# A gated layer of 8 experts: rows beyond two whole pieces packed, and some down products on unsplit operands

## The chip, the cores and the metric

One core of one Trainium2 chip runs the whole kernel in one launch. The metric is device time in microseconds. Before: 599.43 us, the median of three runs (598.75 to 601.22).

## The reference, cut to what matters

Four blocks of a gated cross-attention network over x (1024 tokens of 128 numbers, here kept as 128 partitions by 1024 columns). Each block has an attention-like part and a feed-forward part. The change touches the feed-forward part of the second block, called layer 1 in the code:

```
logits = xt @ Wg.T                       # 8 experts
w, idx = top_k(softmax(logits), 2);  w = w / w.sum()
cw[token, idx] = w                       # 1024 x 8, two non-zero per token
h = silu(xt @ W1[e].T) * (xt @ W3[e].T)  # per expert, 352 hidden rows
y = sum over e of cw[:, e] * (h @ W2[e].T)
x = x + tanh(g_ffn[1]) * y
```

All eight experts are computed for all tokens, and the gate rows (the weights of each expert per token, the tanh factor in them) make the sum.

## The kernel before, in words

Every engine has its own instruction stream, written out by hand, and the streams meet through semaphores. PE multiplies, ScalarE (ACT) and VectorE (DVE) work on what it leaves in PSUM, GpSimd (POOL) does some side work, and SP issues nearly all DMAs on one queue.

**Steps.** The class `Moe` (L41) holds a layer's plan: a list of steps (expert, piece, half). For layer 1 (L100) a piece is 128 hidden rows, the third one 96 (352 = 128 + 128 + 96); a half is 512 tokens. The order is expert by expert: three pieces of the first half, three of the second. Experts 6 and 7 share a tail: both first halves, then both second ones. That is 48 steps. `lag` (L78) gives the step at which so many half-steps have passed since an expert was done, and so times the work on splits, gates and sums.

**A step.** PE's `up` (L717) makes two products (W1, W3) of one piece, each in three passes on split operands: the fp32 value is written as a high part of type fp32r and a low part, and high*high, high*low and low*high are added (`products`, L708, its matmul on L713). Then ACT's `hidden` (L1116, L1132) takes silu of the first into `h_act`, DVE's `product` (L1579, L1586) multiplies by the second, ACT's `high` (L1146) and DVE's `low` (L1600, L1609) split the result, and PE's `down` (L749) multiplies by the piece of W2 in three passes, into the expert's two PSUM banks. PE runs `up` three steps ahead of `down`. `up(s)` waits for `product(s-2)`, since two pairs of PSUM banks alternate.

**Weights.** Two slots in SBUF hold two experts' W1, W3 and W2. SP's `load` (L355, issue on L363) fills a slot once both of the old expert's low parts are made; ACT makes the high part (`split_hi_up` L958, `split_hi_down` L971), DVE the low part (`split_lo` L1544, L1548), at steps set by `next_weights`. The first two experts' low parts are POOL's, in the attention before.

**Gates.** Routing runs on DVE between its first steps; PE turns the weights (`turn_gates`, L780, after down 5), ACT copies them to SBUF, SP writes them to DRAM (L427) and reads each expert's row back to all 128 partitions (`spread`, L382, issue on L384), eight of them, and only then issues the load of expert 4. DVE's `gate` (L1611, L1621) multiplies an expert's output by its row into `y_g`, `accumulate` (L1623, L1629) adds it to x, 1024 columns at once. Experts 6 and 7 go through `finish` (L1551, multiply on L1567, add on L1568) per half. A down product of expert e + 2 waits for the gate of e, which frees its banks.

**The end of the layer.** The next norm's products (L452, L459, L469) stand behind downs 42, 43 and 44, the `features` products of the next block (L646) behind down 46. They wait for the last `product` and for the norm. Then the pair sums begin: ACT's tanh over sums that DVE (L1468) and POOL make. DVE runs the two finishes of the second half between its pair sums (L1434, L1436), and PE's next mean, and ACT's square of it (L915), wait for them.

**Layer 2** behind it has the same up products (L739 to L741), and its down product (L756) is one matmul on fp32 operands that aren't split; the compiler makes it two instructions in the trace.

Of the kernel before, what the change touches and what calls it, by code (L numbers as in the profile page):

```python
# [25 lines left out]
P = 128  # L26
B, S = 16, 64
T = B * S
# [12 lines left out]
class Moe:  # L41
# [4 lines left out]
    def __init__(self, layer, experts, hidden, gated, slots, topk, ahead, orders, routed=None):  # L46
        self.layer, self.experts, self.gated, self.slots, self.topk, self.ahead = layer, experts, gated, slots, topk, ahead
        self.routed = routed or experts
        self.hidden = hidden
        self.chunks = [(f, min(P, hidden - f)) for f in range(0, hidden, P)]  # L50
        self.up = hidden * (2 if gated else 1)
        self.width = self.up + P * len(self.chunks)
        self.steps = []
        for kind, group in orders:
            pieces = range(len(self.chunks))
            if kind == "halves":
                self.steps += [(e, k, t) for t in range(2) for e in group for k in pieces]
            else:
                self.steps += [(e, k, None) for e in group for k in pieces]
# [4 lines left out]
        self.begin = [b - a for a, b in zip(size, self.end)]  # L64

# [34 lines left out]
    Moe(1, 8, 352, True, 2, 2, 3, [("halves", [e]) for e in range(6)] + [("halves", [6, 7])]),  # L100
# [20 lines left out]
def flamingo(nc, a, out):  # L121
    ctx = ExitStack()
    with ctx:
# [97 lines left out]
        table = sb("table", [P, 1])  # L221
        h_part = [h_act[:, i // 2, (i % 2) * HALF:(i % 2 + 1) * HALF] for i in range(4)]
# [21 lines left out]
        def down2(e):  # L244
# [22 lines left out]
              + ["wlu_first"] + (["scaled", "sel"] if m.layer == 2 else ["hi", "lo", "whd", "wld", "wld_first", "gate", "acc"]) + ["xn"] * (m.layer == 3)} for m in MOES]  # L267
# [44 lines left out]
        def acc_bank(m, e):  # L312
            return 4 if m.layer == 2 else 4 + 2 * (e % 2)
# [35 lines left out]
        def _(sp):  # L349
# [5 lines left out]
            def load(m, e):  # L355
# [5 lines left out]
                dst = w_f32[:, u * m.width:(u + 1) * m.width]  # L361
                src = a[f"w{m.layer}"][bass.ds(e, 1)].rearrange("e p w -> (e p) w")
# [22 lines left out]

            for m in MOES:
                if m.layer:

                    last = MOES[m.layer - 1]
                    low_ready(sp, last, last.experts - 1, "u")  # L390
                    if m.layer != 3:
                        low_ready(sp, last, last.experts - 1, "d")
# [35 lines left out]
                sp.wait_ge(once["rows"], 16 * nth(m))  # L428
                for e in range(8):
# [11 lines left out]
        def _(pe):  # L441
# [257 lines left out]
            def moe(m, after={}):  # L699
# [4 lines left out]
                def wap(w, e, lo, size, rows=P):  # L704
                    at_col = (e % m.slots) * m.width + lo
# [11 lines left out]
                def up(step):  # L717
# [3 lines left out]
                    if L == 2 and step == 16:  # L721
                        pe.wait_ge(ln["lo"], 2 * L + 2)
                    if not m.gated:
                        if m.freed(step):
                            pe.wait_ge(s["act"], m.freed(step))
                        f, size = m.chunks[k]
# [17 lines left out]
                    f, size = m.chunks[k]  # L744
                    for i in range(2):
                        mm = products([ps[0:size, 2 * sl + i]], e, i * m.hidden + f, size, P, [n_hi[:, half(t)]], [n_lo[:, half(t)]])
                    mm.then_inc(s["hid"], 1)

                def down(step):  # L749
                    e, k, t = m.steps[step]  # L750
                    acc = acc_bank(m, e)
                    if L == 2:
# [3 lines left out]
                        pe.matmul(ps[:, acc + t], down2(e), h_part[step % 16], start=False, stop=(step + 1 == m.last_of(t))).then_inc(s["h_used"], 1)  # L756
                        return
                    pe.wait_ge(s["lo"], step + 1)
                    if step == m.index(e)[0]:
                        low_ready(pe, m, e, "d")  # L760
                    if step == m.index(e, t)[0]:
                        if e == 1:
                            pe.wait_ge(once["gT"], nth(m))
                        if e >= 2:
                            pe.wait_ge(s["gate"], gates_through(m, e - 2, t))
                    f, size = m.chunks[k]
                    ends = {"first": k == 0, "last": k == len(m.chunks) - 1}
# [1208 lines left out]
```

## Time and profile before

| | |
|---|---|
| median of three runs | 599.43 us |
| the profiled execution, its own time | 601.89 us |
| its span | 600.1 us |
| granted PE clock, mean | 0.99 |
| PE / DVE / ACT busy | 566.8 / 447.4 / 415.2 us |
| this layer's products | from 170.88 to 281 us |
| packets moved by DMA | 40.27 MB, mean 67 GB/s |

The profile is of one execution. Starts are in us from the span's start. Matmuls overlap: the time one costs is the distance from its start to the next one's, less than its own duration. A bracket at a row's end is the engine's idle time before it, and what ended it.

### The profile page before, as it was taken

Reading aid. Unit: us, or ns where it says so; the run is one execution under the profiler, and the core shown is the slowest. Engines: PE = TensorE matmul, PEld = TensorE weight load, DVE = VectorE, ACT = ScalarE, POOL = GpSimd, SP = SyncE. Lnnn points to the kernel's source line nnn. Section 1 sums busy time; section 2 is a strip of 40 time slices with the busy share of each in tenths; the row PEclk is TensorE's granted clock in tenths of the full one; section 3 lists DMA queues with packets and bytes.
Section 4 is the critical chain, followed back from the end, with each engine's and each line's share of the span. In section 5 each row is a group of like instructions: output and inputs, shape, how many; then the busy total and the mean of one; then the engine's idle time right before and its main releaser. Section 6 shows DMA issues by size and latency. Waiting matters only on the chain.

```text
span 600.1 us, 8818 instructions
## 1 busy us (share of the span) xinstructions
PE 566.8 (94%) x3305; PEld 394.1 (66%) x3310; DVE 447.4 (75%) x696; ACT 415.2 (69%) x579; POOL 103.8 (17%) x69
## 2 busy tenths in 40 slices
PE   7999999989999999999896989999998999999997
PEld 5688787656677777775230436566545777888886
DVE  4378987588657898987989676766766847787786
ACT  4798999756755556647999765534513858888885
POOL 5400000001200000003989703200000210000000
PEclk9999999999999999999999799999998999999999
DMA  6207210200200811020000024505510110812100
GB/s 237 71 12 307 71 35 2 74 2 2 76 0 4 317 55 58 2 70 1 5 1 1 1 71 120 164 2 153 163 35 2 37 37 0 301 52 72 37 0 35
DMA packets 16782, 40.27 MB, mean 67 GB/s; under 512 B 1834, under 2 KB 6058, under 8 KB 16740
## 3 DMA queue, kind: packets, MB, share of 16 engines
q1 hardware_dynamic: 16740, 39.71, 19.9%
q8 instruction: 26, 0.43, 0.3%
q14 instruction: 16, 0.13, 0.1%
HBM read 39.01 MB, written 0.70 MB: 66 GB/s over the span
## 4 chain that ended last, share of the span: by engine, by line
PE 71%; DVE 14%; ACT 10%; issue 3%; POOL 1%; DVEq 0%; ACTq 0%; POOLq 0%
PE ps L713 38%; ACT work L1094 6%; PE ps L756 4%; PE ps L452 3%; DVE h_lo L1609 2%; PE ps L469 2%; PE ps L739 2%; PE ps L584 2%; PE ps L741 2%; PE ps L555 2%; PE ps L740 2%; PE ps L569 2%; PE ps L459 2%; PE ps L695 2%; DVE h_act L1586 1%
## 5 line engine op out<-in xcount | busy, mean ns | idle before, releaser
L1609 DVE TENSOR_TENSOR h_lo<-h_act,h_hi 128x512 fp32r<-128x512 f32 (+1 forms) x136 | 118.4, 874 | 39.8 <-ACT h_hi L1139 39.0
L713 PE MATMUL ps<-n_hi,w_hi 128*128 128x512 f32 (+1 forms) x232 | 85.4, 402 | 2.0 <-DVE h_act L1586 1.3
L1139 ACT CAST h_hi<-h_act 128x1024 fp32r<-128x1024 f32 (+1 forms) x88 | 75.3, 856 | 14.6 <-PE ps L713 12.1
L713 PE MATMUL ps<-n_hi,w_lo 128*128 128x512 f32 (+1 forms) x232 | 83.0, 391 | 0.0
L713 PE MATMUL ps<-n_lo,w_hi 128*128 128x512 f32 (+1 forms) x232 | 83.0, 391 | 0.0
L1817 POOL TENSOR_TENSOR rstd<-var_eps,minus_half 128x4 f32<-128x4 f32 x16 | 17.5, 1093 | 319.4 <-DVE var_eps L1273 319.4
L713 PE MATMUL ps<-h_hi,w_hi 128*128 128x512 f32 (+1 forms) x184 | 65.5, 398 | 0.1
L713 PE MATMUL ps<-h_hi,w_lo 128*128 128x512 f32 (+1 forms) x184 | 64.0, 390 | 0.0
L713 PE MATMUL ps<-h_lo,w_hi 128*128 128x512 f32 (+1 forms) x184 | 63.9, 389 | 0.0
L1094 ACT ACTIVATE work<-work,p_rest 128x2048 f32<-128x2048 f32 x31 | 59.5, 1998 | 0.4 <-DVE work L1468 0.4
L1132 ACT ACTIVATE h_act<-ps 128x512 f32<-128x512 f32 (+1 forms) x48 | 28.6, 596 | 40.4 <-PE ps L713 40.4
L1844 POOL TENSOR_TENSOR work<-xc,txt 128x2048 f32<-128x2048 f32 x15 | 53.9, 3624 | 7.9 <-ACT xc L1058 6.7
L713 PEld LDWEIGHTS ps<-n_hi,w_hi 128*128 128x128 f32 (+1 forms) x232 | 42.7, 184 | 13.6 <-DVE h_act L1586 2.1
L713 PEld LDWEIGHTS ps<-n_hi,w_lo 128*128 128x128 f32 (+1 forms) x232 | 42.7, 184 | 10.5
L713 PEld LDWEIGHTS ps<-n_lo,w_hi 128*128 128x128 f32 (+1 forms) x232 | 42.8, 185 | 10.0 <-issue 0.5
L1586 DVE SCALAR_TENSOR_TENSOR h_act<-ps,h_act 128x512 f32<-128x512 f32 (+1 forms) x48 | 32.9, 686 | 16.7 <-ACT h_act L1132 16.5
L1125 ACT ACTIVATE h_act<-ps,p_attn 128x512 f32<-128x512 f32 (+1 forms) x44 | 38.6, 878 | 7.3 <-PE ps L713 6.8
L695 PE MATMUL ps<-work,p_rest 128*32 128x512 f32 x256 | 35.0, 626 | 9.1 <-ACT work L1094 7.9
L1125 ACT ACTIVATE h_act<-ps 128x1024 f32<-128x1024 f32 (+1 forms) x44 | 38.1, 867 | 5.7 <-PE ps L713 5.6
L713 PEld LDWEIGHTS ps<-h_hi,w_hi 128*128 128x128 f32 (+1 forms) x184 | 34.4, 188 | 9.4 <-DVE h_lo L1609 1.2
L713 PEld LDWEIGHTS ps<-h_lo,w_hi 128*128 128x128 f32 (+1 forms) x184 | 34.6, 188 | 7.4 <-issue 0.5
L713 PEld LDWEIGHTS ps<-h_hi,w_lo 128*128 128x128 f32 (+1 forms) x184 | 34.5, 188 | 7.4
(234 smaller groups left out, 1023.7 us busy)
## 6 DMA issues: line engine op xcount, KB each, us to landing
work<-g_rows SPq DMA_DIRECT2D x36, 512.0 KB, 6.4
w_f<-in_w SPq DMA_DIRECT2D x20, 512.0 KB, 3.6
w_f<-in_w SPq DMA_DIRECT2D x8, 544.0 KB, 3.6
work<-in_w SPq DMA_DIRECT2D x2, 512.0 KB, 4.3
work<-g_rows SPq DMA_DIRECT2D x4, 256.0 KB, 9.7
p_rest<-in_p_rest SPq DMA_DIRECT2D x1, 714.0 KB, 9.8
p_attn<-in_p_attn SPq DMA_DIRECT2D x1, 546.5 KB, 6.9
x<-in_xT SPq DMA_DIRECT2D x1, 512.0 KB, 3.6
```

What stands on the lines that cost most here:

```text
L452: pe.matmul(ps[:, LNBANK[j, t][0]], cen_w, x[:, half(t)], start=True, stop=True).then_inc(ln["mean"], 1)
L695: mm = pe.matmul(ps[32 * q:32 * q + 32, DOTS[g // B]], l2pad[:, 31 - g:63 - g], pairs[:, g % 6, q * 512:(q + 1) * 512], start=False, stop= ...
L713: mm = pe.matmul(dst[i], wap(wt, e, lo, size, rows), mv[i], start=(first and c == 0), stop=(last and c == 2))
L756: pe.matmul(ps[:, acc + t], down2(e), h_part[step % 16], start=False, stop=(step + 1 == m.last_of(t))).then_inc(s["h_used"], 1)
L1094: act.activation(pairs[:, g % 6], pairs[:, g % 6], ACT.Tanh, bias=l2b[:, 0:1]).then_inc(x2["tanh"], 1)
L1125: act.activation(places(h_act, m, step), src, ACT.Gelu, **kw).then_inc(s["act"], 1)
L1132: act.activation(h_part[step % parts][0:size], ps[0:size, 2 * (step % 2)], ACT.Silu, **kw).then_inc(s["act"], 1)
L1139: act.copy(places(h_hi, m, step), places(h_act, m, step)).then_inc(s["hi"], 1)
L1586: dve.scalar_tensor_tensor(h, ps[0:size, 2 * sl + 1], b3, h, ALU.add, ALU.mult).then_inc(s["mul"], 1)
L1609: dve.tensor_tensor(lo, src, hi.bitcast(F32), ALU.subtract).then_inc(s["lo"], 1)
L1817: pool.tensor_tensor(rstd[:, r], var_eps[:, r], minus_half[:, r], ALU.pow).then_inc(ln["rstd"], 1)
L1844: pool.tensor_tensor(*sum_of(g, xc[:, half(g // B)]), ALU.add).then_inc(x2["sumB"], 1)
```

## The change

Layer 1's experts keep two whole pieces each (256 hidden rows). The 96 rows left over of experts 0 to 3 are put together to 384 rows, three whole pieces, and so are those of experts 4 to 7: two more "experts", 8 and 9, of three pieces. There are 32 + 12 = 44 steps. Experts 0 and 1 go together now (both first halves, then both second), 2 to 7 one by one, 8 and 9 together at the end.

- A packed piece holds rows of two experts. Its hidden values are multiplied by the gate rows **before** the down product (`gate_packed`, on DVE right after `product`), rows of each expert's gate in the partitions of its hidden rows (`spread_packed`, 12 DMAs into `work`). All packed downs add up in one bank per half, and one `finish` per half adds it to x without a multiply.
- The packed downs, and the down of the second piece and second half of experts 2 to 7, are `unsplit`: one fp32 matmul with the fp32 hidden values and an fp32 copy of W2 (`plain_second`, `plain_rest`, two more DMAs ahead of the load of expert 2). No `high` and no `low` for those 18 steps. Experts 8 and 9 have no split of W2.
- Experts 0 and 1 use one PSUM bank each; ACT copies each half's sum to `y_g` (`keep`), and their gates come at steps 13 and 15, their sums at 14 and 16. All eight experts go through `gate` and `accumulate`.
- SP issues load 4 before it waits for the gates, then sends three gate rows, load 5, three, load 6, two, load 7, four packed pieces' rows, load 8, the last two, load 9.
- What stood at steps 41 to 48 stands four steps earlier, and in the pair sums one finish (expert 9) takes the place of two.

The core of the diff:

```diff
+    def unsplit(self, step):
+        e, k, t = self.steps[step]
+        return self.rest > 0 and (e >= self.routed or e >= self.slots and k == 1 and t == 1)
...
-    def who(self, step, quarters, t=None):
-
-        return [e for e in range(self.experts) if self.lag(e, quarters, t) == step]
+    def next_due(self, step, quarters):
+        return [e + self.slots for e in range(self.experts - self.slots) if self.lag(e, quarters - (self.rest > 0 and e == 0)) == step]
...
-    Moe(1, 8, 352, True, 2, 2, 3, [("halves", [e]) for e in range(6)] + [("halves", [6, 7])]),
+    Moe(1, 8, 352, True, 2, 2, 3, [("halves", [0, 1])] + [("halves", [e]) for e in range(2, 8)] + [("halves", [8, 9])], rest=2),
...
+        def gate_packed(eng, m, step):
+            s, (_, _, t) = mo[m.layer], m.steps[step]
+            c = m.packed(step) % 3 + 3 * (m.steps[step][0] - m.routed)
+            h = h_part[step % 4]
+            eng.wait_ge(s["mul"], step + 1)
+            if c < 4:
+                eng.wait_ge(g_rest_in[0], 16 * 8)
+            else:
+                eng.wait_ge(g_rest_in[1], 16 * 4)
+            return eng.tensor_tensor(h, h, g_rest(c, t), ALU.mult)
...
+            def spread_packed(m, c):
+                if c >= 4:
+                    sp.wait_ge(mo[m.layer]["gate"], 4)
+                for e, p0, p1 in m.owners(c):
+                    sp.dma_start(work[p0:p1, c * T:(c + 1) * T], g_rows[m.layer][e:e + 1, :].broadcast_to([p1 - p0, T])).then_inc(g_rest_in[c // 4], 16)
...
-                for e in range(m.slots, 2 * m.slots):
+                for e in range(m.slots, 2 * m.slots + (m.rest > 0)):
                     load(m, e)
                 sp.wait_ge(once["gT"], nth(m))
...
+                if m.rest:
+                    for gates, weights in ((range(3), 5), (range(3, 6), 6), (range(6, 8), 7)):
+                        for e in gates:
+                            spread(m, e)
+                        load(m, weights)
+                    for c in range(4):
+                        spread_packed(m, c)
+                    load(m, 8)
+                    for c in range(4, 6):
+                        spread_packed(m, c)
+                    load(m, 9)
+                    continue
...
-                    pe.wait_ge(s["lo"], step + 1)
-                    if step == m.index(e)[0]:
+                    if not m.unsplit(step):
+                        pe.wait_ge(s["lo"], m.split(step))
+                    elif e >= m.routed:
+                        pe.wait_ge(s["gated"], m.packed(step) + 1)
+                    else:
+                        pe.wait_ge(s["mul"], step + 1)
...
+                        if m.rest and 4 <= step <= 10:
+                            pe.wait_ge(s["kept"], step // 2 - 1)
...
+                    if m.unsplit(step):
+                        pe.wait_ge(plain_in, 32)
+                        c = (e - m.routed) * len(m.pieces(e)) + k
+                        w = plain_rest[:, c * P:(c + 1) * P] if e >= m.routed else plain_second[:, e * P:(e + 1) * P]
+                        pe.matmul(ps[:, acc_bank(m, e, t)], w, h_part[step % 4], start=ends["first"], stop=ends["last"]).then_inc(s["h_used"], 1)
+                        return
...
+                def keep(i):
+                    step = 2 * i + 1
+                    e, _, t = m.steps[step]
+                    act.wait_ge(s["h_used"], step + 1)
+                    act.copy(y_g[:, e, half(t)], ps[:, acc_bank(m, e, t)]).then_inc(s["kept"], 1)
...
                         if m.gated:
-                            if e == 0 and step == m.lag(0, 7):
-                                gate(0, 0)
-                                gate(0, 1)
+                            if e < m.slots and step == 13 + 2 * e:
+                                gate(e, 0)
+                                gate(e, 1)
                             for t in range(2):
-                                if e and step == m.lag(e, 5, t):
+                                if e >= m.slots and step == m.lag(e, 6 if e == 2 else 5, t):
                                     gate(e, t)
-                            if step == m.lag(e, 6 if e else 8):
+                            if step == (14 + 2 * e if e < m.slots else m.lag(e, 7 if e == 2 else 6)):
                                 accumulate(e)
...
                     if g == 3:
-                        finish(MOES[1], 6, 1)
-                    if g == 5:
-                        finish(MOES[1], 7, 1)
+                        finish(MOES[1], 9, 1)
```

## Rows read from the trace of the kernel before

**Rows 1.** The page's first part: busy us (share of the span), instructions.

```profile
PE 566.8 (94%) x3305; PEld 394.1 (66%) x3310; DVE 447.4 (75%) x696; ACT 415.2 (69%) x579; POOL 103.8 (17%) x69
```

**Rows 2.** Stretches of the layer: us, busy (x instructions) by engine, granted clock, DMA.

```profile
200.00:207.00 7.00, 6.39 (x28) 4.77 (x27) 7.00 (x12) 4.10 (x9) 0.00 (x0) 1.00 1.02 389
207.00:217.00 10.00, 10.00 (x44) 7.77 (x44) 9.04 (x15) 6.08 (x12) 0.00 (x0) 1.00 0.30 104
...
171.00:281.00 110.00, 108.05 (x480) 83.30 (x480) 91.89 (x162) 65.29 (x119) 2.39 (x2) 1.00 0.20 69
```

**Rows 3.** The chain that ended last, 170 to 290 us, its longest piece: start, us, what.

```profile
206.49 45.34 PE ps L713 x195
```

**Rows 4.** PE in order of time: start, us, line, tiles [idle before <-releaser].

```profile
170.88 0.47 PE L713 MATMUL ps<-n_hi,w_hi 128*128 128x512 f32 x1
...
190.25 1.04 PE L780 MATMUL ps<-p_first,rt_w 128*8 128x128 f32 x8 [0.61 <-DVE rt_w L1542]
...
206.49 0.50 PE L713 MATMUL ps<-n_hi,w_hi 128*128 128x512 f32 x1 [0.61 <-DVE h_act L1586]
...
265.95 0.48 PE L713 MATMUL ps<-n_hi,w_hi 128*96 128x512 f32 x1 [0.66 <-DVE h_act L1586]
...
278.57 1.88 PE L646 MATMUL ps<-n,p_rest 128*128 128x512 f32 x4
```

**Rows 5.** The chain in the next layer's loop, 396 to 410 us: start, us, what.

```profile
404.58 0.86 PE ps L756 x2
...
406.82 0.86 PE ps L756 x2
```

**Rows 6.** PE in order of time: one product of the first 512 tokens' mean, at 270 us.

```profile
270.31 1.12 PE L452 MATMUL ps<-x,p_first 128*128 128x512 f32 x2
```

**Rows 7.** DVE in order of time, 203 to 211 us.

```profile
203.22 0.88 DVE L1548 TENSOR_TENSOR w_lo<-w_f,w_hi 128x704 fp32r<-128x704 f32 x1
204.02 1.21 DVE L1629 TENSOR_TENSOR x<-x,y_g 128x1024 f32<-128x1024 f32 x1
205.16 0.68 DVE L1621 TENSOR_TENSOR y_g<-ps,work 128x512 f32<-128x512 f32 x1
205.76 0.68 DVE L1586 SCALAR_TENSOR_TENSOR h_act<-ps,h_act 96x512 f32<-96x512 f32 x1
...
210.03 0.55 DVE L1548 TENSOR_TENSOR w_lo<-w_f,w_hi 128x384 fp32r<-128x384 f32 x1
210.50 0.69 DVE L1621 TENSOR_TENSOR y_g<-ps,work 128x512 f32<-128x512 f32 x1
```

**Rows 8.** PE, ACT and DVE behind the last up pass of one step, at 208 us.

```profile
208.00 0.40 PE L713 MATMUL ps<-h_hi,w_hi 128*128 128x512 f32 x1
...
208.20 0.60 ACT L1132 ACTIVATE h_act<-ps 128x512 f32<-128x512 f32 x1 [0.70 <-PE ps L713]
...
208.83 0.69 DVE L1586 SCALAR_TENSOR_TENSOR h_act<-ps,h_act 128x512 f32<-128x512 f32 x1 [0.60 <-ACT h_act L1132]
```

**Rows 9.** Issues on SP's queue, in order of time.

```profile
192.35 0.29 SPq L427 DMA_DIRECT2D g_rows<-gT  x1
194.15 4.14 SPq L384 DMA_DIRECT2D work<-g_rows  x8
```

**Rows 10.** DMA issues: gate rows (192 to 198 us), loads (198 us, 210 us); KB, us to landing.

```profile
DMA to landing us min/median/max: 3.9/7.5/10.1
...
w_f<-in_w SPq DMA_DIRECT2D x1, 544.0 KB, 10.8
...
w_f<-in_w SPq DMA_DIRECT2D x1, 544.0 KB, 3.6
```

**Rows 11.** DVE and ACT in order of time at the start of the pair sums.

```profile
284.10 0.69 DVE L1567 TENSOR_TENSOR ps<-ps,work 128x512 f32<-128x512 f32 x1
284.82 0.69 DVE L1568 TENSOR_TENSOR x<-x,ps 128x512 f32<-128x512 f32 x1
...
290.38 0.60 ACT L915 ACTIVATE sq<-ps 128x512 f32<-128x512 f32 x1 [0.38 <-PE ps L452]
```

More of the change, by code:

```diff
@@ L64, in __init__, with pieces, up_of, width_of @@
         self.begin = [b - a for a, b in zip(size, self.end)]
+    def pieces(self, e):
+        return [(f, min(P, self.sizes[e] - f)) for f in range(0, self.sizes[e], P)]
+    def up_of(self, e):
+        return self.sizes[e] * (2 if self.gated else 1)
+    def width_of(self, e):
+        return self.up_of(e) + P * len(self.pieces(e))
+    def part_of(self, e, part):
+        first = self.start_of(e)
+        return (first, first + self.up_of(e)) if part == "u" else (first + self.up_of(e), first + self.width_of(e))
+    def start_of(self, e):
+        return max(self.up_of(o) for o in range(self.experts)) - self.up_of(e)
+    def unsplit(self, step):
+        e, k, t = self.steps[step]
+        return self.rest > 0 and (e >= self.routed or e >= self.slots and k == 1 and t == 1)
+    def split(self, step):
+        return len([i for i in range(step + 1) if not self.unsplit(i)])
+    def packed(self, step):
+        first = self.index(self.routed)[0] if self.rest else self.total
+        return step - first if step >= first else None
+    def owners(self, c):
+        rows = P * c + np.arange(P)
+        return [(e, *(np.flatnonzero(rows // self.left == e)[[0, -1]] + [0, 1]).tolist()) for e in sorted(set((rows // self.left).tolist()))]
     def index(self, e, t=None):
@@ L1140, in high @@
                         return
-                    size = m.chunks[m.steps[step][1]][1]
+                    size = m.pieces(m.steps[step][0])[m.steps[step][1]][1]
+                    if m.unsplit(step):
+                        return
                     act.wait_ge(s["mul"], step + 1)
@@ L1216, in moe @@
                         copy_values(0, 2 + step // 4)
+                    if m.rest and step in (5, 7, 9, 11):
+                        keep(step // 2 - 2)
                     if step == 3:
@@ L1586, in product @@
                     dve.scalar_tensor_tensor(h, ps[0:size, 2 * sl + 1], b3, h, ALU.add, ALU.mult).then_inc(s["mul"], 1)
+                    if m.packed(step) is not None:
+                        gate_packed(dve, m, step).then_inc(s["gated"], 1)
                 def scale(step):
@@ L1643, in next_weights @@
                     for after, part in ((up_after, "u"), (down_after, "d")):
-                        for e in m.who(step, after):
-                            if e + m.slots < m.experts:
-                                split_lo(m, e + m.slots, part)
+                        for e in m.next_due(step, after):
+                            if part == "u" or e < m.routed or not m.rest:
+                                split_lo(m, e, part)
                 if L == 2:
```

145 lines of the change are left out of this document (90 added, 55 removed).

## The prediction

> **What bounds the kernel now.** First the shares of busy time: TensorE (PE) 94% of the span, VectorE (DVE) 75%, ScalarE 69% [rows 1]. Then the stretches of this layer, 171 to 281 us: PE is busy 108.05 of 110.00 us at a granted clock of 1.00, DVE 91.89, ScalarE 65.29 [rows 2]. So PE bounds the layer, and DVE is near: 9.04 of 10.00 us between 207 and 217 us, and all of 200 to 207 us, where PE fell to 6.39 of 7.00 [rows 2]. The chain says the same, one piece of 195 passes in 45.34 us: 0.2325 us a pass [rows 3]. The PE lines show the stops: 0.61 us for the routing weights, 0.61 and 0.66 us for a DVE product [rows 4]. Counted from the last pass's slot, not its modelled end, each is 0.17 us more; with a small one the four make 2.6 us. What I call the loop runs from 170.88 to the feature products at 278.57 us, 107.7 us; 429 passes take 99.7 of it.
>
> **Part 1, the passes.** Before: 48 steps; ahead of the feature products lie 48 ups of 6 passes and 47 downs of 3, 429. After: 32 main steps and 12 packed, 44. Ups: 264 passes. Of the 43 downs ahead of the features, 17 are unsplit (11 packed, 6 of the main: second piece, second half, experts 2 to 7), 26 split: 78 passes. So 87 passes go, 87 x 0.2325 = 20.2 us. The 17 unsplit downs come in: the next layer has the same form (fp32 operands, 128x128 by 128x512) at 0.86 us, and its step, six passes and one such product, repeats every 2.24 us [rows 5]; 2.24 less 1.40 is 0.84, so nothing is hidden beside it. 17 x 0.86 = 14.6 us. **Part 1: -5.6 us.** A piece of 96 rows is now 128 rows, but a pass of either takes the same slot.
>
> Bounds of the unsplit product: below 0.84; above 1.12, what one takes in this very layer where the first lies behind an fp32r pass [rows 6]. I take 0.86, from 32 in the same pattern. At 1.12 the part is -1.2 us.
> The Trainium skill, page FP8 and Floating Point Precision, section TensorE Precision Notes, has a true fp32 product as four passes through the array. At the pass of this loop that would be 0.93 us and the part -4.4; the trace shows two records and 0.86, and I go by it.
>
> **Part 2, what DVE and ScalarE must do.** In steady state DVE instructions follow each other every 0.60 us (0.61 at most), a split of 704 columns takes 0.80, of 384 0.47, an accumulation 1.14 [rows 7]; so 512 columns are 0.60, 256 0.34, 768 0.87. Over the layer 22 low parts, 4 products, 2 accumulations and the third columns' splits go, 12 packed gates and a 3-us share of others come: DVE has less to do. But the room per step matters, and experts have 4 steps now, not 6. A round from expert 4 on: four products 2.4, three lows 1.8, splits 0.94, two gates 1.2, accumulation 1.14 = 7.5 us against PE's 3 x 2.09 + 2.26 = 8.5 us. That holds, at 88% as before.
>
> It does not hold in steps 13 to 18, where the gates of experts 0 and 1 are caught up. Step by step: 13: product, low, split u4 0.60, two gates 3.00; 14: product, low, accumulation 2.34; 15: product, low, three gates 3.00; 16: product, split d4, accumulation 2.08; 17: product, low, split, gate 2.40; 18: product, low, gate, accumulation 2.94. Together 15.8 us against 12.7 of PE, 3.1 too much. The lead that absorbs it: from the end of up(s) to the start of up(s+2) PE has a down, an up and a down, 2.8 us; the product of s is done 0.83 + 0.69 us after up(s) [rows 8], so 1.3 us of lead. **The burst stops PE for 3.1 - 1.3 = 1.8, with DVE's own write-out 2.0 us**, in place of the 0.8 and 0.9 us stops at 206 and 265 us and the small one. The routing stop stays (its split moves from step 7 to 6, in front of the same weights; 0.1 us shorter). Up(35), expert 9's first, needs the split of step 33, which now follows a product and a packed gate that waits for it: dependent DVE instructions are 0.72 us apart [rows 11]. 0.83 + 0.72 + 0.60 + 0.94 = 3.1 us against PE's 0.70 + 1.40 + 0.86 = 2.96: 0.2 us. **Stops after 3.0, before 2.6: +0.4 us.** Bounds: -1.5 (burst absorbed) to +2.
>
> Added waits: `kept` before downs 4, 6, 8 and 10 stands in front of PE's queue; the copies lie 1.8 us behind up(5), PE gets there after 4.2 us: nothing. ScalarE gains 22 highs' time and loses 4 copies. `gated` replaces `lo`: same distance. Larger first loads lie in the attention before, where the queue is idle: nothing; with that cover gone, their 3.6 us of landing [rows 10]. The tail has all its steps 4 earlier in the same order: nothing.
>
> **Part 3, SP's queue.** Load 4 is now ahead of the gate rows' write and of eight broadcasts, and so waits for DVE's step 9 (196.0 us by the slots above) in place of the gates at 192.35 [rows 9]. The write then goes at 196.4; before, the first broadcast went 1.8 us behind it [rows 9] and the fastest landed 3.9 us after issue [rows 10]. Behind a load of 384 KB (1.0 us at the 389 GB/s of [rows 2], taken as 1.5 with its start) that makes 196.4 + 1.5 + 1.8 + 3.9 = 203.6 us. The gate that needs it stands at step 13, 203.6 us too. **+0.3 us**, bounds 0 and 3. ScalarE wants load 4 for its split at 200.0 us: 196.0 + 3.6 [rows 10] = 199.6, just in time. Twelve more issues on SP (4.14 us for eight [rows 9], so 6 us) and 3 MB of packed broadcasts lie from step 20 to 32: nothing, 24 us of room.
>
> **Part 4, the pair sums behind.** Two finishes, four instructions of 0.7 us, become one. ScalarE stood 0.38 us for the mean that needed them [rows 11]; it bounds what follows. **-0.4 us**, bounds 0 and -1.
>
> **Sum:** -5.6 + 0.4 + 0.3 - 0.4 = -5.3 us. The profiled execution took 601.89 us (span 600.1); it would be 596.6 (594.8). It stands 0.4% above the median of the three runs, 599.43; the forecast against that is 594.1 us.
>
> **Rivals.** A, the burst is absorbed: ScalarE is freer, DVE's idle time ahead of step 13 is used. -2.0: 592.1. For: the round before had bursts of 2.95 us without a stop. Against: 3.1 us is over twice the lead. Chance 0.15.
> B, DVE becomes the bound of steps 13 to 21: no lead at all, each late product also delays its successor's, 3.1 us and 1 to 2 more of the next rounds: 596 to 597.5. For: DVE full at 200 to 207 us. Against: 8.5 us of PE per 7.5 of DVE behind it. Chance 0.18.
> C, the unsplit product costs its upper bound, so the change does not do what it says: 594.1 + 4.4 = 598.5, no change. For [rows 6], against [rows 5]. Chance 0.07.
> D, slower: load 4 lands late. A load behind a full queue landed after 10.8 us [rows 10]. Then ScalarE stands in its split until 207, 7 us, and the gate rows, queued behind, reach step 13's gate at 212.8, 9.2 us late, which DVE can't make up: 594.1 + 9.2 = 603.3. It decides above 8.3 us of delay to that gate, so 10 us of landing. For: the order on SP. Against: the queue is empty at 196 us; the 10.8 us lay behind 4 MB of broadcasts. Chance 0.05.
> The forecast itself 0.55 (592.9 to 595.6).
>
> **How the numbers follow.** A measurement of this kernel can tell 0.5%, 3.0 us: faster is below 596.4. Forecast and A 0.70, and 0.12 of B: 0.82; same 0.06 of B, C, the rest: 0.13; slower 0.05. The range 591.7 to 598.2 takes in A, B and half of C.
>
> **What would show it.** Right: the loop 102.4 us long; 12 packed products and 6 others at 0.86 us in steps of 2.25; two stops of 0.8 to 1 us some 18 us behind the gates' transposes, released by DVE products; DVE idle again from step 22. Wrong: a product above 0.9 us, a ScalarE wait of its split for a load, a DVE wait of the first gate over 1 us, stops in later rounds. Anything outside this layer and the first pair sums would be a cause I have not seen.

## The result, and the profile after

Faster, inside the range and 0.9 us above the forecast: 595.01 us median of nine runs (forecast 594.1, range 591.7 to 598.2), against 599.43 us before, so the medians are 4.4 us apart. One of the nine runs of each kernel took far longer than the rest (808.48 and 647.52 us), and the ratio leaves it out. The ratio is 0.9911, 95% interval 0.989 to 0.9932; on 599.43 us that is 5.3 us less (4.1 to 6.6). A later series of six runs gave 594.75 us and 0.9899 (0.9866 to 0.9933).

The page's busy shares after, beside [rows 1]. PE lost 7.3 us of work, DVE 7.3, ScalarE 12.6:

```profile
PE 559.5 (95%) x3251; PEld 385.4 (65%) x3256; DVE 440.1 (74%) x684; ACT 402.6 (68%) x559; POOL 101.9 (17%) x69
```

The profiled execution took 593.17 us with a span of 591.4, and the one of before 601.89 with 600.1: 8.7 us apart, more than the medians. So the trace is cut where PE reaches the same instruction in both kernels:

| stretch | before | after | difference |
|---|---|---|---|
| loop: first up pass to feature products | 107.69 | 101.58 | -6.1 |
| from there to the first down product of layer 2 (the pair sums lie here) | 108.59 | 107.45 | -1.1 |
| from there to the first up pass of layer 3 (the rest of layer 2 and an attention) | 107.61 | 106.13 | -1.5 |
| layer 3, to the end | 105.3 | 105.3 | 0.0 |

The loop was forecast 5.3 us shorter at 102.4 us (its sum without Part 4 is -4.9). The second and third rows come up again under the clock.

**The products.** PE in order of time, after (start, us, line, tiles, idle before and what ended it), beside [rows 4]:

```profile
170.92 0.47 PE L801 MATMUL ps<-n_hi,w_hi 128*128 128x512 f32 x1
...
187.95 0.50 PE L801 MATMUL ps<-n_hi,w_hi 128*128 128x512 f32 x1 [0.48 <-DVE w_lo L1662]
...
210.54 0.50 PE L801 MATMUL ps<-n_hi,w_hi 128*128 128x512 f32 x1 [0.64 <-DVE h_act L1702]
...
214.72 0.40 PE L801 MATMUL ps<-h_hi,w_lo 128*128 128x512 f32 x1
215.10 0.47 PE L801 MATMUL ps<-n_hi,w_hi 128*128 128x512 f32 x1
...
217.94 0.50 PE L801 MATMUL ps<-n_hi,w_hi 128*128 128x512 f32 x1 [0.52 <-DVE h_act L1702]
...
246.66 1.02 PE L868 MATMUL ps<-h_act,diag 128*128 128x512 f32 x2
247.79 0.50 PE L801 MATMUL ps<-n_hi,w_hi 128*128 128x512 f32 x1
...
272.50 1.45 PE L734 MATMUL ps<-n,p_rest 128*128 128x512 f32 x3
```

What the reader is to see: the stop at the routing's transposes is gone, and one of about the same size stands a step earlier, at 187.95, where an up waits for the split of its weights. The stops of the DVE burst are at 210.54 and 217.94. Two more have no bracket: 0.38 us instead of 0.23 from 214.72 to 215.10, and the up at 247.79, expert 9's first (line 868 is an unsplit down, line 801 a pass).

The chain that ended last, in the same layer (start, us, what), beside [rows 3, 5]:

```profile
187.29 0.61 DVE w_lo L1662
187.95 2.36 PE ps L801 x9
...
208.00 1.88 DVE y_g L1748 x3
...
217.29 0.61 DVE h_act L1702
...
222.52 7.53 PE ps L801 x33
...
256.19 0.86 PE ps L868 x2
257.05 1.40 PE ps L801 x6
258.44 0.86 PE ps L868 x2
```

Between the two stretches of PE the chain lies on DVE: from 201.42 to 217.90 us it is made of DVE's instructions and short issue times, so for 16.5 us DVE is the bound. An unsplit down costs 0.86 us, and a packed step repeats after 258.44 - 256.19 = 2.25 us, as forecast. And 33 passes take 7.53 us, 0.228 us each, where [rows 3] had 0.2325.

**DVE in the burst.** Products, gates and sums of steps 13 to 19, after; before's rhythm is in [rows 7]:

```profile
201.42 0.69 DVE L1702 SCALAR_TENSOR_TENSOR h_act<-ps,h_act 128x512 f32<-128x512 f32 x1 [1.02 <-ACT h_act L1237]
...
203.25 1.29 DVE L1748 TENSOR_TENSOR y_g<-y_g,work 128x512 f32<-128x512 f32 x2
...
208.00 1.28 DVE L1748 TENSOR_TENSOR y_g<-y_g,work 128x512 f32<-128x512 f32 x2
209.20 0.68 DVE L1748 TENSOR_TENSOR y_g<-ps,work 128x512 f32<-128x512 f32 x1
209.80 0.68 DVE L1702 SCALAR_TENSOR_TENSOR h_act<-ps,h_act 128x512 f32<-128x512 f32 x1
...
217.21 0.68 DVE L1702 SCALAR_TENSOR_TENSOR h_act<-ps,h_act 128x512 f32<-128x512 f32 x1
```

From the product of step 13 to that of step 19 are 217.21 - 201.42 = 15.8 us without a gap. DVE's last idle time before it is 1.02 us. The first gate, at 203.25, waits for nothing: its row had landed at 203.16.

The stretches, beside [rows 2] (us, busy by engine PE, PEld, DVE, ACT, POOL, clock, DMA share, GB/s). The PE loss moved from 200 to 207 us into 207 to 217:

```profile
200.00:207.00 7.00, 7.00 (x31) 5.42 (x30) 5.98 (x11) 3.62 (x7) 0.00 (x0) 1.00 0.94 340
207.00:217.00 10.00, 9.36 (x38) 6.65 (x37) 10.00 (x16) 5.13 (x10) 0.00 (x0) 1.00 0.76 261
```

**SP's queue**, after, beside [rows 9]: load 4, the gate rows' write, then the first three broadcasts.

```profile
195.87 0.33 SPq L427 DMA_DIRECT2D w_f<-in_w  x1
196.25 0.33 SPq L503 DMA_DIRECT2D g_rows<-gT  x1
199.26 1.28 SPq L448 DMA_DIRECT2D work<-g_rows  x3
```

Load 4, of 384 KB, landed 3.2 us after its issue, at 199.04 ([rows 10] had 3.6 for one of 544 KB), and ScalarE's split of it, 0.2 us later, did not wait:

```profile
199.24 0.62 ACT L1071 CAST w_hi<-w_f 128x512 fp32r<-128x512 f32 x1
```

**The pair sums.** The one finish, on DVE, and ScalarE's square, beside [rows 11]. The 0.38 us of idle time before the square is gone:

```profile
278.03 0.68 DVE L1674 TENSOR_TENSOR x<-ps,x 128x512 f32<-128x512 f32 x1
```

```profile
283.84 0.58 ACT L1016 ACTIVATE sq<-ps 128x512 f32<-128x512 f32 x1
```

### The profile page after: what moved, and what is told of

Its sections match the earlier page's. It is cut to its first block, busy times and chain, and to the rows that moved or that the text cites. A ratio compares the mean times of both kernels' runs of the same rounds, so it can differ in the third digit from the quotient of the medians.

```text
span 591.4 us, 8708 instructions
## 1 busy us (share of the span) xinstructions
PE 559.5 (95%) x3251; PEld 385.4 (65%) x3256; DVE 440.1 (74%) x684; ACT 402.6 (68%) x559; POOL 101.9 (17%) x69
## 4 chain that ended last, share of the span: by engine, by line
PE 73%; DVE 14%; ACT 8%; issue 3%; POOL 1%; DVEq 0%; ACTq 0%; POOLq 0%
PE ps L801 36%; ACT work L1197 5%; PE ps L843 4%; PE ps L783 3%; PE ps L557 3%; PE ps L540 3%; DVE h_lo L1729 2%; PE ps L827 2%; PE ps L672 2%; PE ps L829 2%; PE ps L643 2%; PE ps L828 2%; PE ps L868 2%; PE ps L547 2%; PE ps L657 2%
## 5 line engine op out<-in xcount | busy, mean ns | idle before, releaser
L1729 DVE TENSOR_TENSOR h_lo<-h_act,h_hi 128x512 fp32r<-128x512 f32 (+1 forms) x114 | 103.5, 912 | 39.9 <-ACT h_hi L1244 39.1
L801 PE MATMUL ps<-n_hi,w_hi 128*128 128x512 f32 x224 | 86.5, 421 | 2.4 <-DVE h_act L1702 1.2
L801 PE MATMUL ps<-n_hi,w_lo 128*128 128x512 f32 x224 | 79.7, 391 | 0.0
L801 PE MATMUL ps<-n_lo,w_hi 128*128 128x512 f32 x224 | 79.7, 390 | 0.0
L801 PE MATMUL ps<-h_hi,w_hi 128*128 128x512 f32 x162 | 56.3, 396 | 0.1
L801 PE MATMUL ps<-h_hi,w_lo 128*128 128x512 f32 x162 | 55.4, 390 | 0.0
L801 PE MATMUL ps<-h_lo,w_hi 128*128 128x512 f32 x162 | 55.4, 390 | 0.0
L801 PEld LDWEIGHTS ps<-n_hi,w_hi 128*128 128x128 f32 x224 | 42.1, 188 | 17.0 <-issue 3.4
L801 PEld LDWEIGHTS ps<-n_lo,w_hi 128*128 128x128 f32 x224 | 42.1, 188 | 10.7 <-issue 2.9
L801 PEld LDWEIGHTS ps<-n_hi,w_lo 128*128 128x128 f32 x224 | 42.0, 188 | 9.1
L1702 DVE SCALAR_TENSOR_TENSOR h_act<-ps,h_act 128x512 f32<-128x512 f32 x44 | 30.2, 686 | 14.6 <-ACT h_act L1237 14.4
L1582 DVE TENSOR_TENSOR work<-ps,txt 128x2048 f32<-128x2048 f32 x16 | 36.3, 2282 | 1.2 <-PE ps L783 1.1
```

Source lines behind the costliest of these rows:

```text
L801: mm = pe.matmul(dst[i], wap(wt, e, lo, size, rows), mv[i], start=(first and c == 0), stop=(last and c == 2))
L1582: dve.tensor_tensor(*sum_of(g, ps[:, FEAT[g // B]]), ALU.add).then_inc(x2["sumA"], 1)
L1702: dve.scalar_tensor_tensor(h, ps[0:size, 2 * sl + 1], b3, h, ALU.add, ALU.mult).then_inc(s["mul"], 1)
L1729: dve.tensor_tensor(lo, src, hi.bitcast(F32), ALU.subtract).then_inc(s["lo"], 1)
```

## The experiments

Theory P: PE bounds the loop, so every pass counts in full; what the new order adds is the burst of steps 13 to 18 on DVE, and it alone makes the two stops. Rival R: DVE's total work bounds the layer, so that DVE work anywhere in it counts. Each kernel is the changed one with the edit shown. "Loop" is the first row of the table above, in the run's own profile. Ratios are to the kernel before.

### Unsplit downs on PE in place of split ones

The six unsplit downs of experts 2 to 7 go back to three passes, with their high and low parts.

```diff
-        return self.rest > 0 and (e >= self.routed or e >= self.slots and k == 1 and t == 1)
+        return self.rest > 0 and e >= self.routed
```

> The six main downs (second piece, second half, experts 2 to 7) are split again, three passes each; the packed ones stay unsplit. Theory P (PE's passes make the time): 6 x (0.86 - 0.70) = 1.0 us off PE's work, but six lows and six highs come back, four of the lows inside or behind the burst of steps 13 to 18, so the two stops there grow by 1 to 2 us: loop 101.6 plus 0 to 1 us against the changed kernel, total within 1 us of it (594 to 596). Rival R (the gain comes from what VectorE and ScalarE no longer do, not from the passes): a third of the unsplit downs undone gives back a third of the gain, +1.8 us or more, loop 103.4 or more.

Measured: 595.86 us, ratio 0.9928 (0.9909 to 0.9947); loop 102.46 us, 0.9 more. It lies inside P's 0 to 1 us and under R's 103.4. PE's stops behind the routing, as its timeline has them in brackets:

```profile
210.64 0.51 PE L801 MATMUL ps<-n_hi,w_hi 128*128 128x512 f32 x1 [0.68 <-DVE h_act L1702]
...
213.31 0.50 PE L801 MATMUL ps<-n_hi,w_hi 128*128 128x512 f32 x1 [0.30 <-DVE h_act L1702]
...
215.81 0.47 PE L801 MATMUL ps<-n_hi,w_hi 128*128 128x512 f32 x1 [0.15 <-DVE h_act L1702]
...
218.65 0.50 PE L801 MATMUL ps<-n_hi,w_hi 128*128 128x512 f32 x1 [0.52 <-DVE h_act L1702]
...
248.84 0.50 PE L801 MATMUL ps<-n_hi,w_hi 128*128 128x512 f32 x1 [0.76 <-DVE w_lo L1662]
```

One of the six lies inside the burst, and with its low part the stops at 213 and 215 us come. The one at 248.84 is expert 9's first up: 0.9 us from slot to slot, where the changed kernel has 0.4. Six split downs cost PE 6 x (0.86 - 0.69) = 1.0 us less. But the stops of the loop, each counted from slot to slot, sum to 4.2 us here and to 2.7 in the changed kernel, and the first slot behind a stop is some 0.1 us longer than the others, of which there are four more. So these six unsplit downs return about twice what they cost PE, and the loop gains 0.9 by them. What is left of the gain, 5.2 us, comes with the packing (four steps fewer, its downs unsplit) and the new order; no run has the packing alone.

### 24 more passes on PE

From step 20 on, one bf16 product on constants, into a bank not in use, ahead of each up.

```diff
+                    if L == 1 and step >= 20:
+                        keep_busy(1, 2 * sl)
```

> 24 idle bf16 passes, one ahead of each up from step 20 on, each 0.21 us. P: PE bounds these steps, so all of it is on the path: 24 x 0.215 = +5.2 us, less up to 0.3 us taken from stops (loop 106.5 to 106.8 us). R: VectorE bounds the rounds and passes are beside it: under +2 us.

Measured: 598.59 us, ratio 0.998 (0.996 to 1.0001); loop 106.70 us, 5.1 more for 24 passes, 0.213 us each. The chain shows them in line with the rest (L534), with no slack that would swallow them:

```profile
225.89 0.23 PE ps L534
226.12 2.08 PE ps L801 x9
228.20 0.23 PE ps L534
```

That is inside P's 106.5 to 106.8 and far above R's 2 us. This is the plainest test of Part 1: in the rounds behind the burst PE alone is the bound. (The whole grew by 3.6 us by the medians, less than the loop; why the whole can differ from the loop stands under the clock.)

### DVE's sums moved to GpSimd

The eight additions of `accumulate` leave DVE; POOL does them while it has nothing else to do.

```diff
-                            if step == (14 + 2 * e if e < m.slots else m.lag(e, 7 if e == 2 else 6)):
-                                accumulate(e)
...
+            for e in range(8):
+                pool.wait_ge(mo[1]["gate"], gates_through(MOES[1], e, 1))
+                if e:
+                    pool.wait_ge(mo[1]["acc"], e)
+                pool.tensor_tensor(x[:, :], x[:, :], y_g[:, e % 2], ALU.add).then_inc(mo[1]["acc"], 1)
```

> The eight accumulations of 1024 columns go from VectorE to GpSimd, which idles in the loop. P: only the two burst stops (0.64 and 0.52 us, 1.5 us by the passes' slots) can go, since PE bounds elsewhere: -1.5 us against the changed kernel, loop 100.1 us, no stop left but the small one in front of the first split. R: VectorE bounds the loop; 8 x 1.14 = 9.1 us of its work go and the loop falls by 3 us or more. Third: the two engines get in each other's way and VectorE's instructions get longer than 0.68 us: no gain.

Measured: 599.3 us, ratio 0.998 (0.9959 to 1.0002); loop 104.76 us, 3.2 more. Less work on DVE made the loop longer, the third of the outcomes named. POOL's row and DVE's at the same time:

```profile
205.01 2.42 POOL L1998 TENSOR_TENSOR x<-x,y_g 128x1024 f32<-128x1024 f32 x1 [32.27 <-DVE y_g L1748]
```

```profile
204.85 0.69 DVE L1702 SCALAR_TENSOR_TENSOR h_act<-ps,h_act 128x512 f32<-128x512 f32 x1
205.45 2.53 DVE L1729 TENSOR_TENSOR h_lo<-h_act,h_hi 128x512 fp32r<-128x512 f32 x1
207.90 0.68 DVE L1702 SCALAR_TENSOR_TENSOR h_act<-ps,h_act 128x512 f32<-128x512 f32 x1
```

A DVE instruction with both inputs in SBUF (L1729) takes 2.53 us instead of 0.68 when it meets the POOL addition, and ends 0.55 us after it. Each of the eight additions holds one DVE instruction in this way (1.6 to 2.5 us long then), 12 us more in all, where DVE was spared 9.1 us of sums. The product on L1702, one input in PSUM, keeps its mean of 686 ns over the layer while the mean of L1729 goes from 680 to 979 ns. The Trainium skill, page SBUF — State Buffer, section Who interferes with whom, has this rule: a DVE instruction with two SBUF inputs contends with a GpSimd instruction that reads SBUF, one with at most one does not. The trace agrees on both halves. So this run does not test what freeing DVE would bring; it shows that this way of freeing it is closed.

### The packed gates left out

The 12 multiplies of the packed rows by their gate rows are left out, so the output lacks the gate of those rows.

```diff
-                        pe.wait_ge(s["gated"], m.packed(step) + 1)
+                        pe.wait_ge(s["mul"], step + 1)
...
-                    if m.packed(step) is not None:
-                        gate_packed(dve, m, step).then_inc(s["gated"], 1)
```

> The twelve gate multiplies of the packed pieces are left out (so the experts' left-over rows enter ungated); everything else stays. P: they are covered by PE's 2.25 us steps, so 12 x 0.69 us of VectorE's time go and the loop loses only the small stop before expert 9's first up product, 0 to 0.3 us. R: VectorE's new work is on the path: 12 x 0.6 = 7 us or a good part of it.

Measured: 592.75 us, ratio 0.9898 (0.9864 to 0.9933); loop 101.14 us, 0.4 less (P had up to 0.3), though DVE is busy 77.45 us in the loop instead of 85.38. 7.9 us of DVE work are worth 0.4 us: against R. The 0.4 lie at one place, expert 9's first up. With the gate out, the split ahead of it is done sooner:

```profile
248.23 1.02 PE L868 MATMUL ps<-h_act,diag 128*128 128x512 f32 x2
248.68 0.80 PE L801 MATMUL ps<-n_hi,w_hi 128*128 128x512 f32 x1
249.32 0.40 PE L801 MATMUL ps<-n_lo,w_hi 128*128 128x512 f32 x1
```

From the unsplit down to the up's second pass are 1.09 us here; with the gate they are 1.47 (246.66 to 248.13). That 0.38 us is the stop without a bracket shown above.

### Load 4 behind the first spreads

```diff
-                for e in range(m.slots, 2 * m.slots + (m.rest > 0)):
+                for e in range(m.slots, 2 * m.slots):
...
+                        if weights == 5:
+                            load(m, 4)
```

> Load 4 goes back behind the gates' write and the first three broadcasts. P: the order on the queue was nearly free, so the loop stays within 0.7 us of the changed kernel's 101.6: the gate rows come 4 us earlier and nobody waits for them, and load 4 lands at 200 to 201.5 us, up to 1 us late for ScalarE's split of expert 4. R (the queue's order mattered, rival D's mechanism): a ScalarE wait of 2 us or more for the load and a loop above 103.

Measured: 596.59 us, ratio 0.9941 (0.9915 to 0.9968); loop 102.75 us, 1.2 more, above the 0.7 that P allowed and a little under R's 103. The load landed 5.7 us after its issue, behind three broadcasts of 512 KB, and ScalarE stood for it; PE followed:

```profile
202.03 0.62 ACT L1073 CAST w_hi<-w_f 128x512 fp32r<-128x512 f32 x1 [2.28 <-DMA w_f<-in_w]
```

```profile
207.02 0.47 PE L803 MATMUL ps<-n_hi,w_hi 128*128 128x512 f32 x1 [0.76 <-DVE h_act L1704]
```

So the order on SP, load 4 first, is worth 1.2 us, and this is how rival D would have looked: a load that lands 2 us too late already costs a microsecond.

### PE kept busy in the pair sums

Two kernels that put products on constants ahead of pair sums, to see whether the half clock (below) follows from PE's idle time there. Early ones:

```diff
+                    if 1 <= g <= 5:
+                        keep_busy(2 if g in (2, 3) else 3, 3)
```

> Two or three idle bf16 products (0.21 us each) on a free bank in front of the pair sums 1 to 5. In the changed kernel's trace the granted clock stood at half from 288.8 to 292.4 us, after PE had waited for ScalarE, and ScalarE later waited 0.84 us for the second feature product; in the kernel before it stood at 1.00 there. If the lower clock is the cause of that wait, the clock stays at 1.00 there and the wait is gone: -0.8 us in the pair sums' part. If the wait comes from the new order (one finish instead of two), it stays at 0.8 us.

Measured: 595.84 us, ratio 0.993 (0.9908 to 0.9951). No half clock near 288 us in its profile, but the profiles of before and of five other kernels of these experiments had none there either, so it doesn't tell what brings the half clock. What the half clock does there, the profiles together tell: ScalarE's wait for the second feature product is 0.82 to 0.86 us in the four with half the clock between 288 and 295 us (the changed kernel twice, the packed gates left out, the late busy products), under 0.15 in the six of the changed form without it, and 0.38 in this one, with its added products. So that wait goes with the half clock, and the new order alone does not make it. Late ones:

```diff
+                    if 17 <= g <= 24:
+                        keep_busy(3, 2)
```

> Three idle bf16 products on a free bank in front of each of the pair sums 17 to 24, where PE is busy half the time in all profiles. In five of six profiles the granted clock then stood at half for about 3.4 us between 318 and 357 us, once or twice. If that idle time is what lowers the clock, at most one such stretch is left between 300 and 370 us and the part from the feature products to the next layer's first down product, 107.5 to 108.6 us in profiles with two stretches, comes near the 104.9 us that it took in the one profile without any: -1 to -2.5 us. If it is not, nothing changes (or up to +1 us from the products themselves).

Measured: 594.84 us, ratio 0.9916 (0.9888 to 0.9944). The half clock fell at 291 to 294 and 335 to 339 us; the pair sums' stretch was 108.87 us, the longest of all profiles. (The "107.5 to 108.6 us" expected of two such stretches was too narrow: the profile with 24 more passes has two and 106.42 us.) The profile gained nothing, but it is one execution. The granted clock of the nine runs has a mean of 0.993, where the three other kernels of the changed form on the same chip have 0.990, 0.991 and 0.990: a hint, in nine runs, that such stretches became fewer. The time did not fall: two of its runs at a clock of 0.991 took 596.6 and 596.9 us, and the changed kernel's five at that clock 594.0 to 595.0. That idle time is the cause is neither confirmed nor refuted.

### The burst spread out

The first two gate rows are sent before load 4, so expert 0's gate can stand at step 12; the gates of expert 1 at 14, those of expert 2 two steps apart instead of together, the sums at 13, 16 and 19.

```diff
+                            if e == 1:
+                                load(m, 4)
...
-                            if e < m.slots and step == 13 + 2 * e:
+                            if e < m.slots and step == 12 + 2 * e:
...
-                                if e >= m.slots and step == m.lag(e, 6 if e == 2 else 5, t):
+                                if e >= m.slots and step == m.lag(e, 6 - t if e == 2 else 5, t):
...
-                            if step == (14 + 2 * e if e < m.slots else m.lag(e, 7 if e == 2 else 6)):
+                            if step == ((13, 16, 19)[e] if e <= m.slots else m.lag(e, 6)):
```

> The same work in another order: gate rows of experts 0 and 1 are asked for before load 4; gates of expert 0 at step 12, of 1 at 14, sums of 0, 1, 2 at steps 13, 16, 19, second gate of 2 at 16. P (the two stops at 210 and 218 us are the burst's 3.1 us less the lead): no step group is over the lead now (largest lateness 1.35 us against 1.3), so the stops shrink from 1.5 to 0.2 us by the slots: loop 100.3 us, 1.3 below the changed kernel. R: the stops come from somewhere else (the first split, the kept copies) and stay.

Measured: 593.64 us, ratio 0.9889 (0.9852 to 0.9927); loop 99.85 us, 1.7 less. Since its interval overlaps that of the changed kernel, both ran again together:

> The respread spreads and packed gates once more, beside the changed kernel. Theory (the two burst stops are real cost of the changed order): loop 99.9 us, 1.7 us shorter than the changed kernel's, and about 0.988 of the kernel before. Rival (what the loop saves is lost behind it to waits or to the clock): loop 99.9 us but the whole at 0.991, as the changed kernel.

> The changed kernel once more, unaltered, on the same chip as the respread one: loop 101.6 us, the whole 0.991 of the kernel before.

Measured on the same chip: 592.65 us (591.45 to 594.26) and ratio 0.9864 (0.9833 to 0.9896) for the spread one, 594.75 us (593.97 to 595.86) and 0.9899 (0.9866 to 0.9933) for the changed one, six runs each. Loops 99.89 and 101.45 us. In the second profile of the spread kernel only the first of PE's bracketed stops is left in the loop (expert 9's first up still takes its 0.38 us):

```profile
189.88 0.50 PE L803 MATMUL ps<-n_hi,w_hi 128*128 128x512 f32 x1 [0.49 <-DVE w_lo L1664]
```

and its stretch has a full DVE beside a full PE:

```profile
207.00:217.00 10.00, 10.00 (x42) 7.42 (x41) 10.00 (x18) 6.03 (x12) 0.00 (x0) 1.00 0.67 222
```

The medians differ by 2.1 us, the loops by 1.6: what the loop saves is kept. The same DVE work in another order removes both burst stops: the burst was their cause, and not DVE's total, which stayed (85.31 us busy in the loop, 85.38 in the changed kernel). The ratios' intervals overlap, but on this chip five of its six runs lie below the lowest of the changed kernel's six: this version is the fastest of the three. Its load 4 landed 4.6 us after issue and ScalarE waited 1.15 us for it without stopping PE, so it has little left to give there.

## Why the prediction was right

**Part 1, the passes: right.** Forecast -5.6. The unsplit downs cost 0.86 us in the chain and 0.87 from start to start within the repeated step (2.25 less its six passes, 1.38 in the chain). At the mean slot of before, 0.2311 over 408 undisturbed pairs of starts, the 87 passes were 20.1 us; 17 x 0.87 = 14.8 comes back: -5.3. Rival C is out, and so is the 0.93 us for four passes. That figure took the fp32r pass of this loop as the price of each. The bf16 products of the 24 more passes took 0.213 us each, and four of those are 0.85 us, so the four passes of the Trainium skill (page FP8 and Floating Point Precision, section TensorE Precision Notes) are not refuted by the 0.86; only the price per pass was.

One thing was not forecast, a term put at nothing: the slot of the passes that stay. Their mean is 0.2289 us after (297 pairs), and 342 of them save 0.75 us by it. It is no accident of one execution: the ten other profiles of the changed form have means of 0.2285 to 0.2292 (0.9 us in the second profile of the changed kernel). The prediction had "a pass of either takes the same slot", and for a single pass that is nearly so: in before's loop the passes of the pieces of 96 rows have a mean of 0.2304 and the others 0.2314. But the longer slots go with the layer. Layers 0 and 3, all in whole pieces, have 0.2273 and 0.2270 us in the kernel before (353 and 422 pairs), and the same in the one after, and only layer 1, with its pieces of 96 rows, has 0.2311. There the mean slot of an up repeats every three steps, 0.235, 0.231 and 0.232 us, while the ups of the changed kernel's main steps behind the burst have 0.227. So the pieces of 96 rows, or the layout of the weights that goes with them, are the suspects; no run keeps one of them to show it.

**Part 2, DVE: the mechanism right, the size of the lead off.** The burst of 15.8 us came out as 15.8. The two stops come from the steps where they were put and are released by DVE products; they stand 20 and 27 us behind the gates' transposes (forecast: some 18 us). Each counted from slot to slot, the stops are:

| | before | after, forecast | after, measured |
|---|---|---|---|
| routing / weights' split of that round | 0.77 | 0.7 | 0.65 |
| burst | | 2.0 | 0.81 + 0.15 + 0.69 = 1.65 |
| expert 9's first up | | 0.2 | 0.38 |
| stops that the change removes | 0.78 + 0.82 + 0.22 | | |
| sum | 2.6 | 3.0 | 2.7 |

(The forecast's own terms, 0.7 + 2.0 + 0.2, are 2.9 and not the 3.0 that it adds up.) So +0.1 in place of +0.4. The step that was mis-sized is "1.3 us of lead": 3.1 us of excess cost 1.65, so 1.45 were absorbed. Rival A's reason, idle DVE time ahead of step 13, is in the trace as 1.02 us, but that does not by itself carry the burst: 1.6 us went when the burst was spread. How the 1.45 split up between that idle time and the lead, no run shows. Rival B is out: no stops in the later rounds, and 7.9 us less DVE work brought 0.4. The routing stop was forecast to stay at the transposes; it is gone there, and the split that moved in front of them stops an up instead, one step earlier and for nearly as long. So its size was right and its place was not.

**Part 3, SP: 0 in place of +0.3.** The forecast's own times, row and gate both at 203.6 us, give 0; the 0.3 was added on top of them. The write went at 196.25 as forecast (196.4), the first broadcast 3.0 us behind it (forecast 3.3), and it took its 3.9 us: the row landed at 203.16, 0.1 us before the gate wanted it. Load 4, called "just in time", was, and the experiment that delays it shows the price of missing: 1.2 us. Rival D did not happen, since the load landed in 3.2 us on an empty queue.

**Part 4, the pair sums: -0.4 confirmed where it was argued.** The square at 283.84 stands 6.54 us earlier than at [rows 11], the feature products 6.07 us earlier: 0.47 more. All eleven profiles of the changed form have this distance within 0.01 us (11.34 to 11.35 us, 11.81 before), so it repeats; that the missing finish makes it is argued from the idle time of 0.38 us that went, since no run puts the finish back.

**The sum.** Loop: -5.3 - 0.75 + 0.1 = about -6.0 us, where -6.1 was measured and Parts 1 to 3 had -4.9. With Part 4 the work done is 6.5 us shorter, and both ratios hold that (4.1 to 6.6 and 4.0 to 8.0 us). The whole, though, fell by 5.3 us by the first ratio and by 4.4 and 4.7 by the medians. That the forecast of -5.3 came out so near is in part luck: the loop gained 1.2 us more than its parts said, and the runs lost about as much to a lower clock, which the forecast had nowhere.

**The clock, which the forecast left out.** Granted clock by the microsecond in the attention behind layer 2, before (columns as in the stretches):

```profile
455.00:456.00 1.00, 0.65 (x3) 0.65 (x4) 0.97 (x2) 0.00 (x0) 0.30 (x1) 0.76 0.00 0
456.00:457.00 1.00, 1.00 (x7) 1.00 (x6) 0.60 (x1) 0.00 (x0) 0.00 (x0) 0.50 0.00 0
```

after, the same work 8 us earlier, and a stretch in the pair sums:

```profile
449.00:450.00 1.00, 1.00 (x11) 0.95 (x10) 1.00 (x2) 0.21 (x1) 0.00 (x0) 1.00 0.05 16
...
290.00:291.00 1.00, 1.00 (x8) 0.32 (x6) 1.00 (x1) 1.00 (x2) 1.00 (x2) 0.50 0.08 16
```

The clock stood at 0.50, the 1.2 GHz level, for some 3.4 us, from 455.4 us on, after PE had waited 0.89 us for POOL. What it costs, on the same two groups of matmuls in PE's order of time, first before, then after:

```profile
455.35 1.96 PE L469 MATMUL ps<-p_first,rstd 128*128 128x128 f32 x8 [0.89 <-POOL rstd L1817]
457.10 1.92 PE L569 MATMUL ps<-p_first,y_g 128*128 128x128 f32 x8
```

```profile
448.15 1.16 PE L557 MATMUL ps<-p_first,rstd 128*128 128x128 f32 x8 [0.89 <-POOL rstd L1943]
449.15 1.04 PE L657 MATMUL ps<-p_first,y_g 128*128 128x128 f32 x8
```

The same wait stood ahead of both, and only one was followed by half the clock. Where a profile has such a stretch in that attention, the table's row of layer 2 is 107.6 us, and 106.1 where it has none: nine and three of the twelve profiles. The three are the changed kernel's two and that of the late busy products; before has it, but so have the seven other kernels of the changed form. So the 1.5 us of the table is the price of one such stretch and no gain of the change. In the row of the pair sums both profiles have two such stretches; what makes up its -1.1 us beyond the 0.47 of Part 4 is open.

The runs without a profile tell more, since each has its mean granted clock. The kernel before has a mean of 0.9929 over the 57 runs beside the experiments, the changed kernel 0.9899 over its 14. The difference, 0.003, is what one more stretch of 3.4 us at half the clock makes in 593 us, an estimate from the rows above; at the 1.5 us that one costs in the attention, it takes about that much off the gain. Compared at the same clock (the rows mix the chips), the medians are further apart than over all runs:

| granted clock of the run | before | changed | difference |
|---|---|---|---|
| 0.988 | 603.97 (5 runs) | 595.81 (5) | -8.2 |
| 0.991 | 601.14 (15) | 594.77 (5) | -6.4 |
| 0.994 | 599.42 (12) | 593.48 (2) | -5.9 |

So the gain at an equal clock is 5.9 to 8.2 us by these rows, in keeping with the 6.5 us of the loop and Part 4, and the changed kernel's runs spend more time at the lower clock, not less. Seven of its eight edits, too, have means of 0.989 to 0.992, each below the kernel before on the same chip; the late busy products are the exception. Why the new form draws more of it is open.

## What to carry to other kernels

Price a change of instruction count by the slot of the engine that bounds the stretch, and then look in the other engines for the few steps where postponed work is caught up: here 15.8 us of DVE work per 12.7 us of PE cost 1.65 us, though DVE had time to spare over the layer. Spreading that work over neighbouring steps, with the transfers that feed it sent sooner, gives it back (1.6 us). Compare runs at the same granted clock, or stretches of the trace, before a difference of 1 or 2 us is believed. A load that is wanted at a fixed time goes on the queue before broadcasts of half a megabyte each.

## What the runs showed of the hardware that was not expected

- A DVE subtraction or multiplication with both inputs in SBUF that starts during a 2.4 us POOL addition over SBUF ends 0.3 to 0.55 us after it, and so takes up to 2.5 us instead of 0.68; one with an input in PSUM keeps its 0.67 to 0.69 us. Moving the eight additions to POOL cost the loop 3.2 us.
- The granted clock falls to the 1.2 GHz level for about 3.4 us, once to five times in a profile (and in most once more at its very end), in and behind stretches in which PE waits for other engines (pair sums, attention), and at places that differ between profiles of kernels whose code there is the same. In the attention one costs 1.5 us. Filling PE's idle time in part did not remove them. The two profiles of the changed kernel differ by 1.6 us of span, and the second reaches the loop 1.76 us later, with such a stretch at 10.6 to 14.0 us; the loop itself, cut out of the trace, repeats within 0.2 us (101.58, 101.45, and 99.85, 99.89).
- The slot of one pass lies between 0.224 and 0.24 us within a layer at full clock; its mean over the loop was 0.2311 us before and 0.2285 to 0.2292 in eleven profiles of the changed form, and 0.227 in the layers of whole pieces only. What moves it was not tried.
- A load of 384 KB landed 3.2 us after issue on an empty queue, 4.6 us behind two 512 KB broadcasts and 5.7 to 6.4 us behind three.
